# Gated delta-rule recurrence on one core: tokens loaded a round further ahead, another order on TensorE, ScalarE and GpSimd, Gram tiles with step and kind innermost

## The chip, the cores and the metric

One core of a Trainium2 chip runs the whole program. The metric is the device time of one execution in microseconds (us); lower is better. The engines are TensorE (PE; its weight loads are the row PEld), VectorE (DVE), ScalarE (ACT), GpSimd (POOL), and the queue of SyncE (SP), which issues nearly all DMAs.

## The reference, cut to what matters

The program computes four residual blocks on x of shape (4, 1024, 128) in float32: a gated delta rule (phase a), a routed expert FFN (b), banded attention (c), and two layers of local attention with FFN (d). The change touches phase a alone. Its core, for 16 heads with key and value width 64:

```
q, k, v = silu(causal_conv4(x @ W.T))      # 4 taps over time, per channel
a, beta = sigmoid(x @ Wa.T + ba), sigmoid(x @ Wb.T + bb)
def step(S, inp):
    qt, kt, vt, at, bt = inp
    err = jnp.einsum('bhij,bhj->bhi', S, kt) - vt
    S = at[..., None] * S - bt[..., None, None] * (err[..., None] * kt[:, :, None, :])
    o = jnp.einsum('bhij,bhj->bhi', S, qt)
    return (S, o)
# then: o normalised over its 64 values, times sigmoid(x @ Wg.T), times Wo
```

Each of the 1024 steps needs the state S that the step before left, so the recurrence is serial in time.

## The kernel before

**Tiling.** Time is cut into 32 segments of 32 steps (`SEG`), each into two chunks of 16 steps (`CK`). The loop of each engine runs once per segment; such a round s also makes the projections of segment s+1, the normalisation of s-1 and the gate and output of s-2. g = 2s + chunk numbers the chunks. All engines run through fixed lists (`tensor`, `scalar`, `gpsimd`, `vector`, `sync` of `DeltaRule`); semaphores hold them together. Nothing is scheduled at run time: what stands first in an engine's list goes first, and a wait holds all that stands behind it on that engine.

**VectorE's chain.** For each chunk VectorE transposes P2, the products of keys and queries with the past state, out of banks 4 and 5 (L1284), then does steps 1 to 7 (products L1319, sums L1325), transposes the first half's w into `Wt` (L1340), and waits for TensorE's `pe_cross` (L709), which multiplies Wt by the Gram values `Gx` of the first half against the second. It transposes that result into `X` (L1353), does steps 9 to 15, transposes w again (L1381) and forms the outputs `o2` (L1392). Between L1340 and L1353 it places other work: in chunk 0 the reduction of the mean (L1263), the transpose of the decay gates (L1239) and of an older o (L1273); in chunk 1 the reduction of the deviation (L1263) and the transpose of the Gram rows `G1` to `g2` (L1255). At step 4 of chunk 0 it adds half of the state (L1367).

**TensorE.** In a round: `pe_U` (L735; keys times w into the new state; batches 0 and 1, then 2 and 3 after L1284 has emptied banks 4 and 5), `pe_time_rows` (L604), projections of the gates `a` (L569), of `g` (L556), `pe_moment` (L632), `pe_cross` (L709), `pe_turn` (L614), projections of k and q (L556), `pe_past_state` (L672) and `pe_past_chunk` (L691), which together make the P2 of the next chunk, `pe_gram` (L581), `pe_next_gram` (L594), the second cross, the projection of v (L569), `pe_out` (L644), `pe_past_state`, `pe_carry` (L718), `pe_past_chunk`. Projections and Gram products go through a ring of two banks (`take`): the n-th waits until ScalarE has emptied the one two before it.

**ScalarE** empties these banks in the same order. `act_gram` copies each Gram bank three ways: 128 x 256 to `Gn` (L836), 128 x 256 of the second chunk to `G1` (L838) and four times 16 x 256 of the first chunk (L842). `G1` lies as [kind z, step t, head]; one head's steps are 16 elements (64 bytes) apart.

**GpSimd** multiplies the state by the chunk's decays (`pool_decay`, L1004, four quarters), works on the history of w, scales P2 and X (L1079 to L1105), builds running decays (`pool_cumulate`, L1138), and at the round's end prepares the next segment: `pool_gram_rows` (L1162), `pool_prepare` (L1055), `pool_values` (L1155). **SyncE** loads the tokens of segment s+1 (`xseg`, four buffers, L1418) at the start of round s, and spreads the decays over the state's layout (L1437).

Of the kernel before, what the change touches and what calls it, by code (L numbers as in the profile page):

```python
# [442 lines left out]
class DeltaRule:  # L443
# [251 lines left out]
    def pe_cross(self, e, q, s, ch):  # L695
# [25 lines left out]
    def pe_U(self, e, q, s):  # L721
# [3 lines left out]
        for pair in range(0, NB, 2):  # L725
# [14 lines left out]
    def tensor(self, e, q):  # L740
# [9 lines left out]
        for s in range(self.nseg):  # L750
            old, older, nxt, g = s - 1, s - 2, s + 1, 2 * s
            more = nxt < self.nseg
            if old >= 0:
                self.pe_U(e, q, old)
            for n in range(2):
                self.pe_time_rows(e, q, s, n)
            if more:
                for half in range(2):
                    self.pe_project_rows(e, q, "a", nxt, half)
# [6 lines left out]
            if older >= 0:  # L766
                for n in range(2):
                    self.pe_turn(e, q, older, n)
            if more:
                for part in range(2):  # L770
                    self.pe_project(e, q, "k", nxt, part)
                self.pe_project(e, q, "q", nxt, 0)
            self.pe_past_state(e, q, g + 1)
            self.pe_past_chunk(e, q, g + 1)
            if more:
                for part in range(1, 3):
                    self.pe_project(e, q, "q", nxt, part)
                for n in range(2):
                    self.pe_gram(e, q, nxt, n)
            if old >= 0:  # L780
                self.pe_moment(e, q, old, "dev")
            if more:
                for n in range(2):
                    self.pe_next_gram(e, q, s, n)
            self.pe_cross(e, q, s, 1)
            if more:
                for half in range(2):
                    self.pe_project_rows(e, q, "v", nxt, half)
            if older >= 0:
                self.pe_out(e, q, older)  # L790
            if more:
# [34 lines left out]
    def act_gram(self, e, q, s, par):  # L826

        heads = slice(8 * par, 8 * par + 8)
        v = self.held(("gram", s, par)).rearrange("p (r c t z) -> p c r z t", z=2, c=NCK, t=CK)
        dst = self.G1[:, :, :, heads].rearrange("p z t r -> p r z t")  # L830
        q.wait_ge(self.s_full, ("gram", s, par))
        if s:
# [3 lines left out]
        e.activation(self.Gn[0][:, heads, :], self.held(("gram", s, par)).rearrange("p (r x) -> p r x", r=NCT)[:, :, SEG:], ACT.Copy,  # L836
                     scale=1 / 8).then_inc(*self.s_gahead.at((s, par)))
# [40 lines left out]
    def act_gram_bank(self, e, q, g):  # L878
# [6 lines left out]
        e.activation(self.gbank[:, 0:CK - 1, 0, :], self.g2[:, 0, 1:CK, js], ACT.Copy)  # L885
# [2179 lines left out]
```

## Time and profile before

| | us |
|---|---|
| median of 3 runs | 3957.62 (3955.55 to 3961.41) |
| profiled execution | 3969.15, its span 3967.4 |
| busy in the span: PE, PEld | 3272.5, 2459.8 |
| busy: DVE, ACT, POOL | 2960.2, 2058.8, 2234.4 |

A line of the timeline view gives start and length in us, engine, line, operation, output<-inputs, shapes and count; in brackets the idle time of the engine before it and what ended it. "issue" is time in which the engine waited for nothing that the profile shows. Phase a's recurrence lies between about 150 and 2430 us of the span.

### The profile page before, as it was taken

The page shows a single profiled execution, that of the slowest core. Times are in us where ns is not written, and L with a number is a line of the kernel's source. Part 1 is how long each engine was busy: PE and PEld are TensorE (multiplying, and loading weights), DVE is VectorE, ACT ScalarE, POOL GpSimd, SP SyncE. Part 2 cuts the span into 40 slices and gives each one's busy share as a digit, 9 for nine tenths or more (in the row PEclk, how much of TensorE's full clock was granted, in tenths as well). Part 3 has the DMA queues.
Part 4 walks back from the last instruction along what each step waited for, and adds up shares of the span by engine and source line. Part 5 has one row for each costly group of instructions (what it writes and reads, how often), then busy time and mean ns, then how long its engine had stood idle before and what let it go on. Part 6 is the DMA issues. An engine that isn't in the chain of part 4 may idle for free. (4 is left out here: it accounts for less than half of the span.)

```text
span 3967.4 us, 141766 instructions
## 1 busy us (share of the span) xinstructions
PE 3272.5 (82%) x61117; PEld 2459.8 (62%) x61117; DVE 2960.2 (75%) x6533; ACT 2058.8 (52%) x4486; POOL 2234.4 (56%) x2793
## 2 busy tenths in 40 slices
PE   4688888888888888888888874769999889898989
PEld 2567666676676766666667663545666557655765
DVE  4488887877878888788888883147888878847884
ACT  2434444444444444434444432337887789828982
POOL 1367767767676777767767672431101088608860
PEclk8889999889899999889989985789999999999999
DMA  2111111111111111111011113200000011101111
GB/s 74 31 41 39 30 50 31 43 39 29 44 39 43 40 29 45 38 42 38 27 39 37 39 37 107 66 27 2 2 2 2 14 31 39 36 18 31 38 37 27
DMA packets 156019, 141.02 MB, mean 36 GB/s; under 512 B 64977, under 2 KB 108237, under 8 KB 155139
## 3 DMA queue, kind: packets, MB, share of 16 engines
q1 hardware_dynamic: 153090, 129.25, 11.9%
q8 instruction: 482, 7.90, 0.8%
q0 software_dynamic: 2304, 2.71, 0.2%
q14 instruction: 143, 1.16, 0.1%
HBM read 96.12 MB, written 16.82 MB: 28 GB/s over the span
## 5 line engine op out<-in xcount | busy, mean ns | idle before, releaser
L1319 DVE TENSOR_TENSOR a_tmp<-a_h,banks 128x128 f32<-128x128 f32 (+6 forms) x896 | 435.6, 486 | 28.8 <-DVE a_h L1294 0.2
L1325 DVE TENSOR_REDUCE a_h<-a_tmp 128x64 f32<-128x128 f32 (+6 forms) x896 | 432.0, 482 | 8.8
L1004 POOL TENSOR_TENSOR a_st<-a_st,a_ab 128x512 f32<-128x512 f32 x252 | 315.2, 1278 | 0.0
L813 ACT ACTIVATE a_kq<-banks 128x512 f32<-128x512 f32 (+2 forms) x160 | 88.9, 556 | 400.8 <-PE banks L556 400.8
L556 PE MATMUL banks<-a_xseg,a_w_k 128*128 128x128 f32 x2048 | 250.4, 284 | 50.9 <-ACT a_oT L919 33.6
L556 PEld LDWEIGHTS banks<-a_xseg,a_w_k 128*128 128x128 f32 x2048 | 244.3, 200 | 58.2 <-ACT a_oT L919 40.5
L2198 ACT ACTIVATE c_s<-c_s,c_low 128x384 f32<-128x384 f32 (+1 forms) x512 | 266.3, 579 | 18.9 <-DVE c_low L2142 13.5
L1019 POOL TENSOR_TENSOR a_h<-a_h,a_a 128x128 f32<-128x128 f32 (+3 forms) x256 | 141.2, 551 | 226.5 <-DVE a_h L1325 223.3
L2142 DVE CUSTOM_DVE_ANT_0 c_s<-banks,c_band 128x384 f32<-128x384 f32 (+1 forms) x512 | 245.5, 517 | 23.6 <-PE banks L2067 23.6
L2243 POOL TENSOR_TENSOR c_qm<-c_qT,c_heads 128x512 f32<-128x512 f32 x32 | 33.3, 1040 | 396.1 <-PE banks L2067 395.8
L556 PE MATMUL banks<-a_xseg,a_w_q 128*128 128x128 f32 x2048 | 242.8, 275 | 3.3 <-issue 3.3
L569 PE MATMUL banks<-a_w_v,a_xseg 128*32 128x512 f32 x2048 | 240.9, 623 | 1.2 <-ACT a_va L822 1.2
L2081 PE MATMUL banks<-k_ident,c_s 128*128 128x128 f32 x1408 | 216.6, 283 | 28.6 <-ACT c_pt L2205 15.8
L556 PEld LDWEIGHTS banks<-a_xseg,a_w_q 128*128 128x128 f32 x2048 | 233.9, 191 | 6.5 <-issue 3.6
L2081 PEld LDWEIGHTS banks<-k_ident,c_s 128*128 128x128 f32 x1408 | 154.3, 142 | 119.8 <-ACT c_s L2198 113.6
L822 ACT ACTIVATE a_va<-banks 128x512 f32<-128x512 f32 x128 | 138.4, 1108 | 172.1 <-PE banks L569 172.0
L2579 ACT ACTIVATE d_S<-d_S,d_low 128x128 f32<-128x128 f32 x512 | 199.2, 399 | 19.0 <-DVE d_low L2644 18.6
L2428 PE MATMUL banks<-d_wqkv,d_hT 128*128 128x512 f32 x384 | 198.8, 632 | 11.3 <-DVE d_rot L2626 6.8
L709 PE MATMUL banks<-a_wt,a_gx 32*32 32x64 f32 x8192 | 182.3, 259 | 25.9 <-DVE a_wt L1340 18.4
L1323 DVE TENSOR_TENSOR a_h<-a_h,banks 128x32 f32<-128x32 f32 (+6 forms) x640 | 175.1, 274 | 22.0
L709 PEld LDWEIGHTS banks<-a_wt,a_gx 32*32 32x32 f32 x8192 | 168.5, 149 | 36.3 <-issue 31.2
L2719 POOL TENSOR_TENSOR d_sw<-d_raw,d_tab 128x256 f32<-128x256 f32 x256 | 178.4, 729 | 0.0
(326 smaller groups left out, 8961.0 us busy)
## 6 DMA issues: line engine op xcount, KB each, us to landing
a_ab<-decays SPq DMA_DIRECT2D x512, 128.0 KB, 3.0
d_Vs<-d_V SPq DMA_DIRECT2D x128, 128.0 KB, 2.4
sent<-k_nothing SPq DMA_DIRECT2D x40, 64.5 KB, 2.6
b_xe<-sent SPq DMA_DIRECT2D x8, 322.5 KB, 3.5
a_xseg<-xn SPq DMA_DIRECT2D x32, 70.0 KB, 2.5
a_xrow<-in_L_attn_x SPq DMA_DIRECT2D x128, 16.0 KB, 1.8
x<-a_xrow SPq DMA_DIRECT2D x128, 16.0 KB, 2.1
back<-k_nothing SPq DMA_DIRECT2D x32, 64.0 KB, 1.6
```

The costliest lines, as they stand in the source:

```text
L556: t = e.matmul(b[:, m * SW:(m + 1) * SW].rearrange("p (b t) -> p b t", b=NB), self.wT[n][:, j, ct * P:(ct + 1) * P], xs[:, :, off:off + SE ...
L569: t = e.matmul(b[bi * SEG:(bi + 1) * SEG, :], xs[:, bi, off:off + SEG], self.wT[n][:, j, part], start=(j == 0), stop=(j == taps - 1))
L709: t = e.matmul(xb[rows, at:at + DK], self.Gx[rows, :, :, 8 * par + ct].rearrange("p z t -> p (z t)"), self.Wt[rows, x:x + 2, :].rearrange( ...
L1004: e.tensor_tensor(sv, sv, self.ab[:, 8 * n:8 * n + 8, :], ALU.mult).then_inc(*self.s_decay.at((g, n)))
L1319: e.tensor_tensor(prod, both, gram, ALU.mult).then_inc(*step.at((g, t, "product")))
L1325: e.tensor_reduce(self.results(ch, t), prod, AX.X, ALU.add).then_inc(*step.at((g, t, "w")))
L2081: t = e.transpose(b[:, j * P:(j + 1) * P], self.S[u % self.NS][:, j * P:(j + 1) * P], self.c.ident[:])
L2142: e.tensor_tensor_reduce(out=self.S[u % self.NS][:, 0:w], in0=self.c.bank(r)[:, 0:w], in1=self.W.band[:, m0:m0 + w], scale=-HD ** -0.5, sc ...
L2198: e.activation(s[:, 0:w], s[:, 0:w], ACT.Exp, scale=-1.0, bias=self.low[u % self.NS][:, 0:1]).then_inc(*self.s_exp.at(u))
L2428: e.matmul(b, self.hT[:, g * P:(g + 1) * P], self.W.wqkv[:, z * INNER:(z + 1) * INNER], start=True, stop=True).then_inc(*self.s_proj.at((g ...
L2579: t = e.activation(s, s, ACT.Exp, scale=-1.0, bias=self.low[g % 2][:, par, r:r + 1], accum_out=self.rows[g % 2][:, par, r:r + 1])
L2719: e.tensor_tensor(self.heads(sw[:, z, :])[:, :, a * hf:(a + 1) * hf], self.heads(raw[:, z, :])[:, :, (1 - a) * hf:(2 - a) * hf], sn, ALU.m ...
```

## The change

1. **Loads.** SyncE loads segment 1 at once and then segment s+2 in round s, behind the first spread of decays, where it loaded s+1 at the round's start.
2. **TensorE.** The two halves of the `a` projection stand between and behind the two halves of `pe_U`, ahead of the time rows. k's two parts alternate with `pe_turn`; `pe_past_state` of the second chunk goes ahead of the first part of q. The deviation's moment goes ahead of the Gram product; `pe_out` and the second cross go ahead of `pe_next_gram`.
3. **ScalarE** follows with the same order.
4. **Layout.** `G1`, `Gx` become [head, t, z] and `g2` [t, z, column], `X` [.., t, z]: ScalarE writes runs of 32, and the cross reads its 32 weights as one run. VectorE's L1255 reads heads 32 elements apart.
5. **GpSimd.** All four decays of the second chunk stand ahead of `pool_cross`; two of them stood behind it. Two steps of `pool_cumulate` move from ahead of it to behind `pool_query`.

```diff
-            self.G1, self.g2 = sb("g1", [P, 2, CK, H0]), sb("g2", [P, 2, CK, SEG])
-            self.Gx, self.X = sb("gx", [P, 2, CK, H0]), sb("cross", [P, 32, 2 * CK])
+            self.G1, self.g2 = sb("g1", [P, H0, CK, 2]), sb("g2", [P, CK, 2, SEG])
+            self.Gx, self.X = sb("gx", [P, H0, CK, 2]), sb("cross", [P, 32, CK, 2])
...
-                    t = e.matmul(xb[rows, at:at + DK], self.Gx[rows, :, :, 8 * par + ct].rearrange("p z t -> p (z t)"),
+                    t = e.matmul(xb[rows, at:at + DK], self.Gx[rows, 8 * par + ct].rearrange("p t z -> p (t z)"),
...
             if old >= 0:
-                self.pe_U(e, q, old)
+                self.pe_U(e, q, old, (0,))
+            if more:
+                self.pe_project_rows(e, q, "a", nxt, 0)
+            if old >= 0:
+                self.pe_U(e, q, old, (2,))
+            if more:
+                self.pe_project_rows(e, q, "a", nxt, 1)
             for n in range(2):
                 self.pe_time_rows(e, q, s, n)
-            if more:
-                for half in range(2):
-                    self.pe_project_rows(e, q, "a", nxt, half)
...
             self.pe_cross(e, q, s, 0)
-            if older >= 0:
-                for n in range(2):
+            for n in range(2):
+                if more:
+                    self.pe_project(e, q, "k", nxt, n)
+                if older >= 0:
                     self.pe_turn(e, q, older, n)
+            self.pe_past_state(e, q, g + 1)
             if more:
-                for part in range(2):
-                    self.pe_project(e, q, "k", nxt, part)
                 self.pe_project(e, q, "q", nxt, 0)
-            self.pe_past_state(e, q, g + 1)
             self.pe_past_chunk(e, q, g + 1)
             if more:
                 for part in range(1, 3):
                     self.pe_project(e, q, "q", nxt, part)
-                for n in range(2):
-                    self.pe_gram(e, q, nxt, n)
             if old >= 0:
                 self.pe_moment(e, q, old, "dev")
             if more:
                 for n in range(2):
-                    self.pe_next_gram(e, q, s, n)
+                    self.pe_gram(e, q, nxt, n)
+            if older >= 0:
+                self.pe_out(e, q, older)
             self.pe_cross(e, q, s, 1)
             if more:
+                for n in range(2):
+                    self.pe_next_gram(e, q, s, n)
                 for half in range(2):
                     self.pe_project_rows(e, q, "v", nxt, half)
-            if older >= 0:
-                self.pe_out(e, q, older)
...
-        v = self.held(("gram", s, par)).rearrange("p (r c t z) -> p c r z t", z=2, c=NCK, t=CK)
-        dst = self.G1[:, :, :, heads].rearrange("p z t r -> p r z t")
+        v = self.held(("gram", s, par)).rearrange("p (r c x) -> p c r x", r=NCT, c=NCK)
+        dst = self.G1[:, heads].rearrange("p r t z -> p r (t z)")
...
             if more:
-                for n in range(2):
+                for n in range(4):
                     self.pool_decay(e, q, g, n)
-                self.pool_cumulate(e, q, nxt, 3, 5)
             self.pool_cross(e, q, s, 1)
             self.pool_first_half(e, q, s, 1)
             if more:
                 self.pool_past(e, q, s)
-                for n in range(2, 4):
-                    self.pool_decay(e, q, g, n)
             self.pool_query(e, q, s, 1)
             if more:
-                self.pool_cumulate(e, q, nxt, 5, HC)
+                self.pool_cumulate(e, q, nxt, 3, HC)
...
-        rows = self.G1[:].rearrange("p z t (h o) -> p (z t) h o", o=1).broadcast_to([P, 2 * CK, H0, 2])
-        e.transpose(self.g2[:].rearrange("p z t j -> p (z t) j"), rows).then_inc(*self.s_g2.at(s))
+        rows = self.G1[:].rearrange("p (h o) t z -> p (t z) h o", o=1).broadcast_to([P, 2 * CK, H0, 2])
+        e.transpose(self.g2[:].rearrange("p t z j -> p (t z) j"), rows).then_inc(*self.s_g2.at(s))
...
         self.load(e, 0)
+        self.load(e, 1)
         self.put_decays(e, q, 0)
         self.spread_decays(e, q, 0)
         for s in range(self.nseg + 2):
-            if s + 1 < self.nseg:
-                if s >= 3:
-                    q.wait_ge(self.s_full, ("g", s - 3, 1))
-                self.load(e, s + 1)
             if s >= 2:
                 self.get_rows(e, q, s - 2)
             self.fill.piece(e, s)
             if s < self.nseg:
                 self.spread_decays(e, q, 2 * s + 1)
+            if s + 2 < self.nseg:
+                if s >= 2:
+                    q.wait_ge(self.s_full, ("g", s - 2, 1))
+                self.load(e, s + 2)
             if s + 1 < self.nseg:
                 self.put_decays(e, q, s + 1)
                 self.spread_decays(e, q, 2 * s + 2)
```

The other edits follow from these: ScalarE's list, and the views of `g2` and `X` in the new layouts with the same elements.

## Rows read from the trace of the kernel before

**Rows 1.** The page, busy us (share of the span) xinstructions

```profile
PE 3272.5 (82%) x61117; PEld 2459.8 (62%) x61117; DVE 2960.2 (75%) x6533; ACT 2058.8 (52%) x4486; POOL 2234.4 (56%) x2793
```

**Rows 2.** Windows view, 30 rounds: length, busy us by engine, PEclk, DMA share, GB/s

```profile
218.10:2341.70 2123.60, 1769.41 (x44976) 1417.29 (x44965) 1731.89 (x3210) 931.86 (x1581) 1521.19 (x2036) 0.92 0.13 38
```

**Rows 3.** Waits of VectorE from 160 to 2400 us: total us, times, longest

```profile
DVE a_cross L1353 <- PE banks L709: 117.8, 35, 4.3
DVE a_g L1255 <- ACT a_g L842: 75.6, 31, 3.8
DVE a_p L1284 <- PE banks L691: 74.9, 33, 4.3
DVE a_mom L1263 <- PE banks L632: 61.1, 27, 5.2
```

**Rows 4.** Timeline of VectorE, chunk 1 of round 12, chunk 0 of round 13

```profile
1030.47 1.25 DVE L1284 STREAM_TRANSPOSE a_p<-banks 128x1024 f32<-128x1024 f32 x1 [2.48 <-PE banks L691]
...
1040.13 2.05 DVE L1340 STREAM_TRANSPOSE a_wt<-a_h 128x1024 f32<-128x1024 f32 x1
...
1044.67 1.25 DVE L1255 STREAM_TRANSPOSE a_g<-a_g 128x1024 f32<-128x1024 f32 x1 [2.41 <-ACT a_g L842]
1049.40 1.25 DVE L1353 STREAM_TRANSPOSE a_cross<-banks 128x1024 f32<-128x1024 f32 x1 [3.49 <-PE banks L709]
...
1064.14 2.46 DVE L1392 TENSOR_TENSOR a_o<-a_p,a_h 128x512 f32<-128x512 f32 x1
1066.70 1.25 DVE L1284 STREAM_TRANSPOSE a_p<-banks 128x1024 f32<-128x1024 f32 x1
...
1082.72 0.29 DVE L1263 TENSOR_REDUCE a_mom<-banks 128x32 f32<-128x128 f32 x1 [3.06 <-PE banks L632]
...
1085.21 1.21 DVE L1353 STREAM_TRANSPOSE a_cross<-banks 128x1024 f32<-128x1024 f32 x1
...
1098.71 1.10 DVE L1392 TENSOR_TENSOR a_o<-a_p,a_h 128x512 f32<-128x512 f32 x1
1101.21 1.25 DVE L1284 STREAM_TRANSPOSE a_p<-banks 128x1024 f32<-128x1024 f32 x1 [1.40 <-PE banks L691]
```

**Rows 5.** Timeline of TensorE in the same stretch

```profile
1029.80 0.63 PE L691 MATMUL banks<-a_wt,a_gn 32*32 32x64 f32 x27 [1.39 <-issue]
1030.36 5.62 PE L556 MATMUL banks<-a_xseg,a_w_q 128*128 128x128 f32 x48
...
1045.70 3.64 PE L709 MATMUL banks<-a_wt,a_gx 32*32 32x64 f32 x128
...
1063.17 2.02 PE L691 MATMUL banks<-a_wt,a_gn 32*32 32x64 f32 x128
...
1068.01 1.98 PE L735 MATMUL banks<-a_wt,a_kt 32*64 32x64 f32 x64 [1.72 <-DVE a_p L1284]
...
1075.04 3.40 PE L569 MATMUL banks<-a_w_a,a_xseg 128*32 128x512 f32 x16 [1.48 <-DMA a_xseg<-xn]
...
1082.61 2.06 PE L709 MATMUL banks<-a_wt,a_gx 32*32 32x64 f32 x128
```

**Rows 6.** Timeline of ScalarE, one Gram bank emptied

```profile
1037.84 0.39 ACT L836 ACTIVATE a_gn<-banks 128x256 f32<-128x256 f32 x1 [1.30 <-PE banks L581]
1038.12 0.62 ACT L838 ACTIVATE a_g<-banks 128x256 f32<-128x256 f32 x1
1038.78 2.48 ACT L842 ACTIVATE a_g<-banks 16x256 f32<-16x256 f32 x4
```

**Rows 7.** Timeline of GpSimd, second half of chunk 1

```profile
1042.63 2.48 POOL L1004 TENSOR_TENSOR a_st<-a_st,a_ab 128x512 f32<-128x512 f32 x2
...
1050.73 0.57 POOL L1092 TENSOR_TENSOR a_cross<-a_cross,a_dk 128x128 f32<-128x128 f32 x1 [4.32 <-DVE a_cross L1353]
...
1063.66 2.39 POOL L1155 TENSOR_TENSOR a_bv<-a_bv,a_beta 128x1024 f32<-128x1024 f32 x1
```

**Rows 8.** Windows view, TensorE alone, during the cross of 1045.70 us

```profile
1045.70:1049.30 3.60, 3.60 (x138) 0.50 0.02 5
```

More of the change, by code:

```diff
@@ L719, in pe_carry, with pe_U @@
                      start=True, stop=False).then_inc(*self.s_carried.at((s, n)))
-    def pe_U(self, e, q, s):
+    def pe_U(self, e, q, s, pairs):
         q.wait_ge(self.s_evac, ("rows", s, 1))
         q.wait_ge(self.s_wt, 2 * s + 1)
-        for pair in range(0, NB, 2):
+        for pair in pairs:
             if pair:
@@ L835, in act_gram @@
             q.wait_ge(self.s_p, 2 * s - 1)
-        e.activation(self.Gn[0][:, heads, :], self.held(("gram", s, par)).rearrange("p (r x) -> p r x", r=NCT)[:, :, SEG:], ACT.Copy,
-                     scale=1 / 8).then_inc(*self.s_gahead.at((s, par)))
+        e.activation(self.Gn[0][:, heads, :], v[:, 1], ACT.Copy, scale=1 / 8).then_inc(*self.s_gahead.at((s, par)))
         e.activation(dst, v[:, 1], ACT.Copy, scale=-1 / 8).then_inc(*self.s_gwhole.at((s, par)))
@@ L952, in scalar @@
                     self.act_project_rows(e, q, "a", nxt, half)
+            for n in range(2):
+                self.act_time_rows(e, q, s, n)
             if older >= 0:
@@ L955, in scalar @@
                     self.act_gate(e, q, older, n)
-                for n in range(2):
+            for n in range(2):
+                if more:
+                    self.act_project(e, q, "k", nxt, n)
+                if older >= 0:
                     self.act_affine(e, q, older, n)
             if more:
-                for part in range(2):
-                    self.act_project(e, q, "k", nxt, part)
                 self.act_project(e, q, "q", nxt, 0)
@@ L971, in scalar @@
                     self.act_gram(e, q, nxt, n)
+            if older >= 0:
+                self.act_out(e, q, older)
+            if more:
                 for n in range(2):
@@ L1104, in pool_query @@
         q.wait_ge(self.s_cross, (g, "decayed"))
-        e.tensor_tensor(of_q[:, :, last], of_q[:, :, last], self.X[:, :, CK + last], ALU.subtract).then_inc(*self.s_pq.at(g))
+        e.tensor_tensor(of_q[:, :, last], of_q[:, :, last], self.X[:, :, last, 1], ALU.subtract).then_inc(*self.s_pq.at(g))
     def pool_gate(self, e, q, s, half):
@@ L1159, in pool_gram_rows @@
         for ch in range(NCK):
-            v = self.g2[:, 0, :, ch * CK:(ch + 1) * CK]
+            v = self.g2[:, :, 0, ch * CK:(ch + 1) * CK]
             bc = self.beta8[:, s * SEG + ch * CK:s * SEG + (ch + 1) * CK].rearrange("p (t o) -> p t o", o=1).broadcast_to([P, CK, CK])
             e.tensor_tensor(v, v, bc, ALU.mult).then_inc(*self.s_bg.at((s, ch, "beta")))
-            flat = self.g2[:].rearrange("p z t j -> p z (t j)")
-            own = ch * CK + SEG + 1
+            flat, row = self.g2[:].rearrange("p t z j -> p (t z j)"), 2 * SEG
+            of_k, of_q = row + ch * CK + 1, SEG + ch * CK + 1
             q.wait_ge(self.s_bg, (s, ch, "beta"))
-            e.memset(flat[:, 0, own:own + (CK - 2) * (SEG + 1) + 1:SEG + 1], 1.0).then_inc(*self.s_bg.at((s, ch, "one")))
-            e.memset(flat[:, 1, own - SEG:own - SEG + (CK - 2) * (SEG + 1) + 1:SEG + 1], 0.0).then_inc(*self.s_bg.at((s, ch)))
+            e.memset(flat[:, of_k:of_k + (CK - 2) * (row + 1) + 1:row + 1], 1.0).then_inc(*self.s_bg.at((s, ch, "one")))
+            e.memset(flat[:, of_q:of_q + (CK - 2) * (row + 1) + 1:row + 1], 0.0).then_inc(*self.s_bg.at((s, ch)))
     def gpsimd(self, e, q):
@@ L1352, in dve_cross @@
             q.wait_ge(self.s_pq, g - 1)
-        e.transpose(self.X[:], self.c.bank(6, 2).rearrange("p (x i) -> p i x", i=32)).then_inc(*self.s_xt.at(g))
+        e.transpose(self.X[:].rearrange("p i t z -> p i (t z)"), self.c.bank(6, 2).rearrange("p (x i) -> p i x", i=32)).then_inc(*self.s_xt.at(g))
         q.wait_ge(self.s_xt, g)
```

15 lines of the change are left out of this document (5 added, 10 removed).

## The prediction

> **What bounds it now.** I read the page's busy line first [rows 1]: TensorE 3272.5 and VectorE 2960.2 us lead, but these are sums over four phases, and the change touches one. The windows view of 30 rounds of it [rows 2] gives 2123.60/30 = 70.8 us a round, VectorE busy 1731.89/30 = 57.7, TensorE 59.0 at a mean granted clock of 0.92, GpSimd 50.7, ScalarE 31.1. So nothing is saturated: the round is a serial chain through VectorE, and what counts is what VectorE waits for. The waits view [rows 3] names four: 117.8 us for the cross, 75.6 for ScalarE's Gram copies, 74.9 for the past chunk, 61.1 for the mean: 329.4 us in 31 rounds, 10.6 a round. The VectorE timeline shows where they lie. Call the starts of L1284 and L1353 D0, X0 in chunk 0 and D1, X1 in chunk 1. Chunk 1 of round 12 [rows 4]: D1 = 1030.47 after 2.48 us of waiting, X1 = D1 + 18.93, of which 2.41 + 3.49 are waits, next D0 = D1 + 36.23. Chunk 0 of round 13: X0 = D0 + 18.51 with 3.06 of waiting for the mean, D1 = D0 + 34.51 with 1.40. The pattern repeats in all middle rounds; the mean's wait swings from 0.5 to 5.2.
>
> **The change, part by part.**
>
> *D0 to X0.* TensorE reaches the mean late: it stands 1.72 us before the second half of U and 1.48 before the `a` rows, which last 3.40, for a DMA [rows 5]. Between U's halves half of the `a` rows (3.40/2 = 1.7) now fills the gap, and tokens issued a round earlier have long landed: together some 3.2 us, against a wait of 3.06. ScalarE's copies out of the ring come in the same new order, so nothing queues in front of them. With the mean early, VectorE's own work sets X0: 18.51 - 3.06 = 15.45. The mean wait (61.1/30 = 2.0 a round) goes. What is late next is the cross: it can't start before L1340 ends, at about D0 + 12.9, and if the clock has fallen in TensorE's new gap before it, it takes 3.64 as in the other chunk and not the 2.06 of this one [rows 5], and X0 slips to D0 + 16.6. I take half of that: **-2.05 + 0.5**. SyncE's added wait (for an old g) holds only the load, the decays' write and the spreads behind it; those wait for GpSimd 39 us at worst anyway, so nothing.
>
> *X0 to D1.* VectorE needs 14.6 us from X0 to be free (1098.71 + 1.10 - 1085.21) [rows 4]. The past chunk starts when L1381 ends, X0 + 12.8, and takes some 2.05, so X0 + 14.85 is possible, a wait of 0.25. It was 2.48 at 1030.47 (about 2.3 on average): 1.39 of "issue" inside the past chunk [rows 5], where 256 small products with their weight loads follow on each other, and the rest of 0.84 by TensorE coming late out of k, q and past state. Now q's first part (1.95) stands between the two, as the carry does ahead of the other chunk, whose past chunk runs its 128 products without such a stop in 2.02 at 1063.17 [rows 5]. With the gaps above filled and k alternating with the turns, TensorE is no longer late. From 2.3 to between 0.25 and 1.6 (the stop stays); I take 0.65: **-1.65**.
>
> *D1 to X1.* ScalarE's Gram bank takes 3.42 now (0.28 + 0.66 + 2.48) [rows 6]. The copy to `Gn`, of the same 256 elements in runs, lasts 0.39 and the next starts 0.28 behind it, where the scattered one lasts 0.62. At that pace a bank is 0.28 + 0.41 + 4 x 0.31 = 1.9 to 2.0; bounds are 3.42 (no gain) and 1.6. From D1: q's parts end at 5.5 [rows 5], the moment 2.05 later, the Grams at 8.5 and 9.45, ScalarE's copies at 10.7 and 12.7 against 14.15 now. That is where VectorE, free at D1 + 11.9, waits 0.8 and no longer 2.4. L1255 (1.25) then ends at 14.0. The cross today starts at 15.2, behind the next Grams, for which ScalarE's copies must have emptied both banks, and at a granted clock of 0.50 takes 3.64 [rows 5, 8]. Ahead of it now stand only Grams and out (2.05), dense work up to D1 + 11.5; it starts with L1340's end at 11.8 and ends at 13.9 warm, 15.4 at half clock. X1 = 14.0 to 15.4 for 18.93; I take 14.3: **-4.6**. L1255 reads heads 128 bytes apart now. The transpose of the cross, with a source stepped as widely but in a bank, takes 1.25, L1340, which writes that way, 2.05 [rows 4]: a price of 0 to 0.8; it is nearer to L1353, as a read, and I put it at nothing.
>
> Here a rule bears. ScalarE's steps of 64 bytes cost 0.62 for 0.39 [rows 6]. The Trainium skill (SBUF — State Buffer, Door 1: The DMA port swizzle) says that SBUF has 16-byte lines, that each access crossing into a new one pays, and that two hits per line are wanted. By it the copies gain, the trace agrees, but L1255 would pay; with L1340's 2.05 X1 is 14.8 and the total 15 us higher. It reads each element twice, which may be the two hits.
>
> *X1 to the next D0.* VectorE needs 14.75 to the start of L1392; that takes 2.46 for 1.10 elsewhere, ending 0.55 behind GpSimd's L1155 (1063.66 + 2.39) [rows 4, 7]. GpSimd is what is late next. It is free of second-half work at D1 + 12.15 and today idles 4.32 us before L1092 [rows 7]. Now four decays (4 x 1.25) end at D1 + 17.2, the cross product is ready at 18.25, and step 12 on VectorE asks for it at X1 + 5.0 = 19.3: covered by 1.0. The rest of its list up to L1155's end is as now, 1050.73 to 1065.98 less two decays plus two cumulates: 15.25 - 2.5 + 1.35 = 14.1. So L1155 ends at D1 + 31.3, and L1392, asked for at 29.05, ends at 31.9 rather than the 31.5 of today's spacing: **+0.4**. ScalarE's copies of v were ready 3.9 us before VectorE took them (1058.26 to 1062.13); the next Grams, about 1.9 of TensorE, now come between cross and v and leave 2.0 of that. The root, behind out and next Grams on ScalarE, is done about 1 us before L1268 asks, an estimate from the same spacings.
>
> *Sum.* -2.05 + 0.5 - 1.65 - 4.6 + 0.4 = -7.4 a round, 63.4 us for 70.8. Rounds 0 to 30 have it: 31 x 7.4 = 229. The last has no next segment, and phases b to d are as before. Against the profiled execution 3969.15 - 229 = 3740; it lies 11.5 above the median of the runs, so I put **3957.6 - 229 = 3729 us**. Floor: all 10.6 of waits but 0.25 + 0.8 a round go, 9.5 x 31 = 295, 3663.
>
> **Rivals.**
> 1. *GpSimd takes VectorE's place.* Its list from D1 + 12.15 on has no idle left. If VectorE's two-input instructions and its own hold each other up as L1392 shows, its end slips by some 2 us: +62, 3791. For: the 2.46 and a cover of only 1.0 at step 12. Against: 4.32 idle today is more than what moves ahead. The Trainium skill (SBUF — State Buffer, Who interferes with whom) tells of a lock for whole instructions between GpSimd and a VectorE instruction with two SBUF inputs; the trace agrees by the 1.36 us of L1392.
> 2. *The copies don't speed up* (what costs isn't the step). Then the Grams are out at D1 + 15.5, X1 = 16.75, 2.45 x 31 = 76 more: 3805. Against: rows 6.
> 3. *TensorE binds in part*: cold crosses in both chunks (0.6 and 1.1 more than taken) and the stop that stays (1.0): 2.7 x 31 = 84, 3813. For: two stretches at half clock are there now. Against: they follow gaps, and the gaps are filled.
> 4. *Slower: TensorE's clock.* At full clock its list is some 57 us a round. If the mixed small products kept a share f of it at 1.2 GHz, the round would be 57 x (1 + f): it decides from f = 0.24, 70.8 us. With a third it is 76, +5.2 x 31: 4119. Against: filling gaps has raised the clock in every dense stretch here.
>
> **How the numbers follow.** Forecast (within 3663 to 3760) 0.60; rival 1 0.14; rival 2 0.06; rival 3 0.12; rival 4 0.03; a loss elsewhere that eats all of it 0.02; better than the floor, by VectorE's instructions meeting GpSimd's less, 0.03. The range 3655 to 3840 leaves out rival 4, half of the better case and what rivals 1 to 3 give together. A measurement of this kernel tells 0.2% (8 us) from no change: faster 0.94, within 0.02, slower 0.04.
>
> **What would show it.** Right: the waits of L1353, L1255, L1284 and L1263 for TensorE and ScalarE fall from 329 to some 90 us; L838 and L842 at 0.38; the cross of chunk 1 at clock 1.00; no DMA wait of the `a` rows; GpSimd's idle before L1092 near nothing. Wrong: L1255 at 2 us; L1319 at step 12 waiting for L1094; L1294 waiting for L1155; the clock of the window below 0.85.

## The result, and the profile after

The changed kernel takes **3811.05 us** (median, 3801.64 to 3818.85) beside 3956.59 for the kernel before on the same chips: a ratio of 0.9632, 95% interval 0.9606 to 0.9658, or 146 us less. Forecast were 3729 in a range of 3655 to 3840: the sign, the range and most of the mechanism held, but over a third of the forecast gain is missing, and the time lies above the 3663 to 3760 to which the prediction gave its main chance of 0.60. The profiled execution took 3810.68 with a span of 3808.9; the profiled kernel before had 3967.4.

The windows view, 30 rounds from D0 of round 1 to D0 of round 31, as in [rows 2] (length, busy us of each engine, granted clock, DMA share, GB/s):

```profile
214.90:2185.10 1970.20, 1721.63 (x45024) 1363.01 (x45024) 1768.69 (x3209) 852.69 (x1581) 1536.13 (x2036) 0.94 0.14 41
```

A round is 1970.20/30 = 65.7 us for 70.8. The reader should see two things. ScalarE is busy 79 us less and TensorE 48 less, as wanted. But VectorE, with the same instructions, is busy **36.8 us more** (1768.69 for 1731.89): some of them have become longer.

The waits view of VectorE, 160 to 2300 us (us in total, times, longest), against [rows 3]:

```profile
DVE a_cross L1353 <- PE banks L709: 61.2, 43, 3.8
DVE a_g L1255 <- ACT a_g L843: 22.3, 31, 2.0
DVE a_st L1367 <- issue: 20.1, 9, 3.2
...
DVE a_p L1284 <- PE banks L691: 17.8, 28, 2.0
DVE a_mom L1263 <- PE banks L632: 15.6, 3, 14.3
DVE a_mom L1268 <- ACT a_mom L899: 7.1, 8, 1.3
```

The four old waits fell from 329.4 to 116.9 us, of which 14.3 is one wait after the last round: 212 us less. Only 158.5 of the span was gained. The difference is in new waits (L1367 20.1, L1268 7.1, and L1247 5.6 for ScalarE's copies of v) and in the longer instructions. The lines view by shape shows those (busy us, mean ns | idle before), first before, then after:

```profile
L1358 DVE TENSOR_TENSOR a_h<-a_p,a_cross 128x128 f32<-128x128 f32 x64 | 27.4, 429 | 2.3
L1289 DVE TENSOR_TENSOR a_p<-a_p,a_dk 128x128 f32<-128x128 f32 x64 | 20.1, 314 | 2.2
L1355 DVE TENSOR_TENSOR a_cross<-a_cross,a_dk 128x128 f32<-128x128 f32 x64 | 18.7, 292 | 2.2
```

```profile
L1358 DVE TENSOR_TENSOR a_h<-a_p,a_cross 128x128 f32<-128x128 f32 x64 | 43.2, 675 | 2.2
L1289 DVE TENSOR_TENSOR a_p<-a_p,a_dk 128x128 f32<-128x128 f32 x64 | 35.3, 552 | 2.2
L1355 DVE TENSOR_TENSOR a_cross<-a_cross,a_dk 128x128 f32<-128x128 f32 x64 | 32.9, 514 | 2.2
```

The same work costs 15.8 + 15.2 + 14.2 = 45 us more; other instructions became a little shorter, which leaves the 36.8. VectorE's timeline of chunk 1 in round 16 shows where (start, length), and GpSimd's beside it shows why:

```profile
1231.76 1.25 DVE L1284 STREAM_TRANSPOSE a_p<-banks 128x1024 f32<-128x1024 f32 x1
1233.05 1.12 DVE L1289 TENSOR_TENSOR a_p<-a_p,a_dk 128x128 f32<-128x128 f32 x1
...
1246.41 1.25 DVE L1353 STREAM_TRANSPOSE a_cross<-banks 128x1024 f32<-128x1024 f32 x1 [0.58 <-PE banks L709]
1247.70 0.89 DVE L1355 TENSOR_TENSOR a_cross<-a_cross,a_dk 128x128 f32<-128x128 f32 x1
1248.62 1.26 DVE L1358 TENSOR_TENSOR a_h<-a_p,a_cross 128x128 f32<-128x128 f32 x1
...
1264.84 1.25 DVE L1284 STREAM_TRANSPOSE a_p<-banks 128x1024 f32<-128x1024 f32 x1
```

```profile
1231.06 2.96 POOL L1116 TENSOR_TENSOR a_y<-a_oT,a_og 128x512 f32<-128x512 f32 x2
...
1244.71 5.03 POOL L1007 TENSOR_TENSOR a_st<-a_st,a_ab 128x512 f32<-128x512 f32 x4
```

L1289 ends at 1234.17, 0.15 after GpSimd's gate products (1231.06 + 2.96); L1358 ends at 1249.88, 0.14 after the four decays (1244.71 + 5.03 = 1249.74). All three have both inputs in SBUF. In the kernel before GpSimd was idle when L1355 and L1358 came (L1092 waited 4.32 us there [rows 7]), and L1289 of chunk 1 came when the gate products were over: it took 0.30 us on average, and now 0.81.

The table gives the four parts of a round as means of rounds 1 to 30, worked out from the timeline view of VectorE of each profile by the starts of L1284 (D0 in chunk 0, D1 in chunk 1) and L1353 (X0, X1). The forecast row is the row of before with the terms of the prediction's sum; the kernels below the changed one are those of the experiments:

| us | X0 - D0 | X0 to D1 | X1 - D1 | X1 to D0 | round |
|---|---|---|---|---|---|
| before | 17.51 | 16.95 | 18.96 | 17.36 | 70.8 |
| forecast | 15.95 | 15.3 | 14.3 | 17.8 | 63.4 |
| **changed** | 16.82 | 15.27 | 14.99 | 18.59 | 65.7 |
| layout_only | 17.00 | 16.75 | 16.72 | 17.53 | 68.0 |
| order_only | 16.65 | 15.40 | 16.41 | 17.48 | 65.9 |
| old_last | 16.36 | 15.25 | 16.77 | 17.22 | 65.6 |
| old_first | 16.47 | 15.02 | 15.05 | 18.51 | 65.1 |
| old_loads | 20.84 | 14.95 | 15.06 | 18.57 | 69.4 |
| old_gpsimd | 16.76 | 15.11 | 14.94 | 17.65 | 64.5 |
| three_decays | 16.55 | 15.17 | 14.83 | 18.30 | 64.9 |
| centre_early | 16.78 | 15.85 | 14.34 | 18.42 | 65.4 |
| both | 16.62 | 15.98 | 14.50 | 18.18 | 65.3 |
| shift64 | 16.75 | 15.37 | 14.70 | 18.67 | 65.5 |
| add_late | 16.19 | 15.07 | 14.99 | 18.64 | 64.9 |
| best | 16.52 | 15.05 | 15.00 | 17.30 | 63.9 |

The decisive column is the last but one: X1 came 4 us earlier, and the way from there to D0 became 1.2 us longer. By instruction, in us a round: L1358 +0.52, L1355 +0.47, the wait of L1268 +0.22 and that of L1247 +0.19, less 0.26 of L1392.

### The profile page after: what moved, and what is told of

The parts are those of the page before. It is cut to its first block and busy times, and to the rows that moved or that the text cites. A ratio compares the mean times of both kernels' runs of the same rounds, so it can differ in the third digit from the quotient of the medians.

```text
span 3808.9 us, 141737 instructions
## 1 busy us (share of the span) xinstructions
PE 3221.9 (85%) x61117; PEld 2401.6 (63%) x61117; DVE 2996.8 (79%) x6533; ACT 1974.1 (52%) x4486; POOL 2251.0 (59%) x2793
## 3 DMA queue, kind: packets, MB, share of 16 engines
HBM read 96.12 MB, written 16.82 MB: 30 GB/s over the span
## 5 line engine op out<-in xcount | busy, mean ns | idle before, releaser
L1319 DVE TENSOR_TENSOR a_tmp<-a_h,banks 128x128 f32<-128x128 f32 (+6 forms) x896 | 435.4, 486 | 28.8 <-DVE a_h L1294 0.2
L556 PE MATMUL banks<-a_xseg,a_w_k 128*128 128x128 f32 x2048 | 260.6, 287 | 26.6 <-DMA a_xseg<-xn 18.2
L569 PE MATMUL banks<-a_w_v,a_xseg 128*32 128x512 f32 x2048 | 263.0, 658 | 7.3 <-issue 7.0
L709 PE MATMUL banks<-a_wt,a_gx 32*32 32x64 f32 x8192 | 156.2, 236 | 129.5 <-DVE a_wt L1340 110.0
L709 PEld LDWEIGHTS banks<-a_wt,a_gx 32*32 32x32 f32 x8192 | 143.5, 119 | 142.5 <-issue 141.4
## 6 DMA issues: line engine op xcount, KB each, us to landing
sent<-k_nothing SPq DMA_DIRECT2D x40, 64.5 KB, 2.5
```

What stands on the lines that cost most here:

```text
L556: t = e.matmul(b[:, m * SW:(m + 1) * SW].rearrange("p (b t) -> p b t", b=NB), self.wT[n][:, j, ct * P:(ct + 1) * P], xs[:, :, off:off + SE ...
L569: t = e.matmul(b[bi * SEG:(bi + 1) * SEG, :], xs[:, bi, off:off + SEG], self.wT[n][:, j, part], start=(j == 0), stop=(j == taps - 1))
L709: t = e.matmul(xb[rows, at:at + DK], self.Gx[rows, 8 * par + ct].rearrange("p t z -> p (t z)"), self.Wt[rows, x:x + 2, :].rearrange("p h i ...
L1319: e.tensor_tensor(prod, both, gram, ALU.mult).then_inc(*step.at((g, t, "product")))
```

## The experiments

**Theory (lock).** The waits went about as forecast, and most of what is missing was lost where VectorE's instructions with two SBUF inputs now meet GpSimd's: the one that comes second is held until the other has ended. **Rivals:** TensorE's order or its stops took it; or GpSimd's list as a whole binds.

layout_only, order_only, old_last and old_gpsimd ran on one chip, three_decays, centre_early, both and old_loads on a second, shift64, old_first, add_late and best on a third, so within such a group the times can be compared directly. shift64 is the changed kernel but for some products ahead of the first round, and stands for it on its chip (3808.16 us, 3802.82 to 3811.19).

### Layout alone, order alone

layout_only is the kernel before with the new layouts of `G1`, `Gx`, `g2` and `X`; order_only is the changed kernel with the old ones.

```diff
-            self.G1, self.g2 = sb("g1", [P, H0, CK, 2]), sb("g2", [P, CK, 2, SEG])
+            self.G1, self.g2 = sb("g1", [P, 2, CK, H0]), sb("g2", [P, 2, CK, SEG])
```

> The kernel before with nothing but the new layout of the Gram tiles and of X. Theory A (VectorE's chain sets the time, and the layout takes the wait for the Gram copies by itself): ScalarE's copies fall to 0.38 us each, the next Grams and so the cross of chunk 1 start earlier too, X1 falls from D1 + 18.9 to between 14.4 and 15.9, mean wait and chunk 0 stay: -3.5 us a round, about 3850 us. Theory B (the order of TensorE's last part is what brings X1 down): X1 stays above 17, 3900 us or more. L1255 stays at 1.25 us by the first, goes to 2.0 if wide steps in SBUF cost a transpose.

Measured: 3881.93 us, ratio 0.9833 (0.9812 to 0.9854). In the changed kernel the copies L839 and L843 take 0.38 and 0.37 us for 0.63 and 0.60, and L1255, which now reads at 128 bytes a step, still 1.25. The wait for the copies nearly vanishes with the layout alone, but the one for the cross stays at 112.7:

```profile
DVE a_cross L1352 <- PE banks L709: 112.7, 35, 4.7
DVE a_p L1283 <- PE banks L691: 63.7, 32, 3.8
DVE a_mom L1262 <- PE banks L632: 45.9, 26, 3.7
DVE a_g L1254 <- ACT a_g L841: 5.4, 8, 1.2
```

X1 is D1 + 16.72: between what the two theories said, and the 3850 us was too low by 32.

> The changed kernel with the old layout. The Gram copies last 3.4 us a bank again, so L1255 ends at about D1 + 16.8 and X1 is there, 1.9 us later than in the changed kernel. Lock theory (VectorE's L1355 and L1358, two inputs in SBUF, are held by GpSimd's decays, which end at D1 + 17.5): they come behind the decays now and fall back to 0.29 and 0.43, which gives 1.4 us back: 0.5 us a round more than the changed kernel, about 3825 us. Without the lock (TensorE or fetch stops took the missing gain): the full 1.9 a round, about 3870 us.

Measured: 3815.85 us, ratio 0.9655 (0.963 to 0.968), within the error of the changed kernel. The Grams' copies cost 96.1 us of waiting again, and X1 is 1.4 later, where 1.9 was expected. But L1355 and L1358 come when the decays are over:

```profile
1250.07 1.25 DVE L1256 STREAM_TRANSPOSE a_g<-a_g 128x1024 f32<-128x1024 f32 x1 [2.98 <-ACT a_g L844]
1251.24 1.21 DVE L1354 STREAM_TRANSPOSE a_cross<-banks 128x1024 f32<-128x1024 f32 x1
1252.48 0.29 DVE L1356 TENSOR_TENSOR a_cross<-a_cross,a_dk 128x128 f32<-128x128 f32 x1
1252.81 0.43 DVE L1359 TENSOR_TENSOR a_h<-a_p,a_cross 128x128 f32<-128x128 f32 x1
```

and X1 to D0 is 17.48 for 18.59. So 1.4 us gained by the layout and 1.1 us lost to GpSimd are the same microsecond: the new layout, worth 1.7% alone, adds next to nothing on top of the order. The lock theory's 3825 was missed by 9 us, the rival's 3870 by 54.

### TensorE's last part as before

```diff
+            if more:
+                for n in range(2):
+                    self.pe_gram(e, q, nxt, n)
             if old >= 0:
                 self.pe_moment(e, q, old, "dev")
             if more:
                 for n in range(2):
-                    self.pe_gram(e, q, nxt, n)
+                    self.pe_next_gram(e, q, s, n)
+            self.pe_cross(e, q, s, 1)
+            if more:
+                for half in range(2):
+                    self.pe_project_rows(e, q, "v", nxt, half)
             if older >= 0:
                 self.pe_out(e, q, older)
-            self.pe_cross(e, q, s, 1)
             if more:
-                for n in range(2):
-                    self.pe_next_gram(e, q, s, n)
-                for half in range(2):
-                    self.pe_project_rows(e, q, "v", nxt, half)
```

(ScalarE's `act_out` goes back behind v too.)

> The changed kernel with the last part of TensorE's and ScalarE's round as before (Gram, deviation, next Gram, cross, v, out). Theory A (with the fast copies this order hardly matters): next Gram waits for ScalarE until D1 + 11.4, the cross ends at 14.4 to 15.9, X1 like the 15.0 of the changed kernel, 3800 to 3835 us. Theory B (the order is what counts): X1 near 17 to 19, 3880 us or more.

Measured: 3808.97 us, ratio 0.9633 (0.9607 to 0.966): no different from the changed kernel, as theory A had it in total. Its reason was wrong, though: X1 - D1 is 16.77 and not 15. The cross is waited for longer, and most of what this costs comes back behind X1, 17.22 for 18.59, where the decays are out of the way (the rest lies in D0 to X0, 16.36 for 16.82):

```profile
DVE a_cross L1355 <- PE banks L709: 131.2, 51, 4.4
```

It is the same exchange as in order_only.

### GpSimd's list as before

```diff
             if more:
-                for n in range(4):
+                for n in range(2):
                     self.pool_decay(e, q, g, n)
+                self.pool_cumulate(e, q, nxt, 3, 5)
             self.pool_cross(e, q, s, 1)
             self.pool_first_half(e, q, s, 1)
             if more:
                 self.pool_past(e, q, s)
+                for n in range(2, 4):
+                    self.pool_decay(e, q, g, n)
             self.pool_query(e, q, s, 1)
             if more:
-                self.pool_cumulate(e, q, nxt, 3, HC)
+                self.pool_cumulate(e, q, nxt, 5, HC)
```

> The changed kernel with GpSimd's list of before: two decays and two steps of the running decays ahead of the cross product, two decays behind. Lock theory: GpSimd is idle when L1355 and L1358 come, they last 0.29 and 0.43 and not 0.89 and 1.26; X1 to the start of L1392 falls from 16.2 to 14.8, -1.2 to -1.4 us a round, about 3770 us: faster than the changed kernel. Rival (the decays ahead of the crossing help, or GpSimd's whole list binds): 3811 or slower.

Measured: 3777.43 us, ratio 0.9578 (0.955 to 0.9606): undoing this part of the change makes it faster. The interval just touches that of the changed kernel; on the same chip all four times (3774.00 to 3793.22) lie below those of old_last (3795.34 to 3811.04) and order_only. The same place in VectorE's and GpSimd's timelines:

```profile
1227.73 0.29 DVE L1358 TENSOR_TENSOR a_cross<-a_cross,a_dk 128x128 f32<-128x128 f32 x1
1228.06 0.60 DVE L1361 TENSOR_TENSOR a_h<-a_p,a_cross 128x128 f32<-128x128 f32 x1
```

```profile
1224.74 2.50 POOL L1007 TENSOR_TENSOR a_st<-a_st,a_ab 128x512 f32<-128x512 f32 x2
1227.20 1.31 POOL L1141 TENSOR_TENSOR a_dc<-a_dc,a_a 128x128 f32<-128x128 f32 x2
```

VectorE's two products (L1358 and L1361 here) take 0.89 us together for 2.15. They still meet the running decays, but each of these lasts 0.66 us, where a decay of the state lasts 1.25: who has to wait, waits for a short one. Over 30 rounds the two give 0.85 us a round.

Another 0.48 comes from L1392 (L1395 here), whose mean in chunk 1 falls from 2.20 to 1.72, and this shows the lock from both sides. In the changed kernel GpSimd's L1158 starts 0.08 us after VectorE's L1247, whose result it reads, has ended, in all 30 rounds, and L1392, which comes 0.71 us later, ends 0.55 us after L1158. VectorE itself releases the instruction that then blocks it; round 16:

```profile
1260.53 1.21 DVE L1247 STREAM_TRANSPOSE a_bv<-a_va 128x1024 f32<-128x1024 f32 x1
1262.54 2.19 DVE L1392 TENSOR_TENSOR a_o<-a_p,a_h 128x512 f32<-128x512 f32 x1
```

```profile
1261.62 0.30 POOL L1060 COPY a_dk<-a_beta 128x64 f32<-128x64 f32 x1
1261.83 2.36 POOL L1158 TENSOR_TENSOR a_bv<-a_bv,a_beta 128x1024 f32<-128x1024 f32 x1
```

This also answers the rival that GpSimd's whole list binds: L1158 waits for VectorE there, with GpSimd idle for up to 2.4 us before it. With GpSimd's old list VectorE comes first in 12 of 30 rounds. L1395 then takes 0.69 to 0.78, and GpSimd's instruction is the one that is stretched (0.83 for 0.30). Round 4:

```profile
466.19 0.69 DVE L1395 TENSOR_TENSOR a_o<-a_p,a_h 128x512 f32<-128x512 f32 x1
```

```profile
466.22 0.83 POOL L1060 COPY a_dk<-a_beta 128x64 f32<-128x64 f32 x1
466.94 2.37 POOL L1158 TENSOR_TENSOR a_bv<-a_bv,a_beta 128x1024 f32<-128x1024 f32 x1
```

Some of it is lost again: the past chunk is waited for 0.26 us longer at D0, so X1 to D0 is 0.94 shorter and not 1.3.

> The changed kernel with three of chunk 1's decays ahead of GpSimd's cross product and one behind. Lock theory: the third decay ends about when L1353 does, so L1355 and L1358 fall from 0.74 and 0.92 to 0.29 and 0.43, GpSimd's list stays as long and as dense: 3770 to 3785 us, like the kernel with GpSimd's old list. Rival (the two steps of the running decays, not the decays, made the difference there): 3805 to 3811 us.

Measured: 3790.03 us, ratio 0.9607 (0.9572 to 0.9643), between the two expectations. L1358 is back at 0.43 (mean over chunk 1), L1355 still at 0.69: in the rounds in which the cross comes late both are free (0.29 and 0.42 in round 15, X1 at D1 + 17.3), in the others the third decay still reaches into L1355. The interval overlaps that of the changed kernel, so by its time alone this run would not decide. Its durations show that the fourth decay was what held L1358. They also show where this went: L1392 of chunk 1 now starts within 0.1 us of L1158 in most rounds, mostly second, and takes 2.47 for 2.20, so X1 to D0 is only 0.3 shorter.

### Moving GpSimd's centring into its idle time

```diff
             if old >= 0:
                 self.pool_clear(e, q, old)
+                for n in range(2):
+                    self.pool_centre(e, q, old, n)
             self.pool_cross(e, q, s, 0)
...
-            if old >= 0:
-                for n in range(2):
-                    self.pool_centre(e, q, old, n)
```

> The changed kernel with GpSimd's two centring products in its idle time ahead of chunk 0's cross product. Lock theory: the gate products end 2.5 us earlier and no longer meet L1289 of chunk 1, which falls from 0.78 to 0.30 us; L1392 of chunk 0 may meet the gates instead: -0.3 to -0.5 us a round, 3795 to 3802 us. Rival (GpSimd's list doesn't matter there): 3811 us.

Measured: 3806.42 us, ratio 0.9659 (0.9617 to 0.9701): nothing gained. L1289 of chunk 1 is at 0.29 as expected. But GpSimd's centring often still runs when L1355 and L1358 of **chunk 0** come (in round 4 both are held until a centring product ends). These two, 0.29 and 0.43 in the changed kernel, have means of 0.53 and 0.72; X0 to D1 is 15.85 for 15.27, X1 - D1 14.34 for 14.99. The meeting was moved, not removed.

> Both edits of GpSimd's list, three decays ahead and centring early, in the changed kernel. If the two lock costs add: 3755 to 3770 us. If VectorE is then stopped by something else (the root, v, the past chunk): 3775 to 3785 us.

Measured: 3796.69 us, ratio 0.9616 (0.9578 to 0.9655). Slower than the 3775 to 3785 of the worse of the two expectations, and no faster than three_decays alone; L1355 and L1358 of chunk 0 are held as in centre_early (0.58 and 0.82).

### The loads as before

```diff
+            if s + 1 < self.nseg:
+                if s >= 3:
+                    q.wait_ge(self.s_full, ("g", s - 3, 1))
+                self.load(e, s + 1)
             if s >= 2:
                 self.get_rows(e, q, s - 2)
```

(and the early load of segment 1 and that of s+2 go)

> The changed kernel with the loads of the kernel before: segment s+1 loaded at the start of round s. The first half of the a rows stands ahead of the second half of U now, so its wait for the load holds U, and with it VectorE's L1367 at step 4, which asks at D0 + 4.7. The load lands near D0 + 8 (issued behind the output rows): 3 to 5 us a round, 3900 to 3960 us. Rival (a load has landed in time anyway, or VectorE isn't held): 3811 to 3830 us.

Measured: 3930.36 us, ratio 0.9949 (0.9925 to 0.9972). The waits of VectorE, then of TensorE:

```profile
DVE a_st L1367 <- issue: 158.5, 30, 7.8
```

```profile
PE banks L569 <- DMA a_xseg<-xn: 160.3, 31, 7.8
```

The 160 us that the `a` rows wait for the DMA reach VectorE whole, through the half of U behind them. With this order the early load is worth some 120 us, and without it the change is nearly nothing. With the old order it had 44 us of DMA wait on TensorE to remove; no run has the early load alone.

### TensorE's first part as before, with the early loads

```diff
-                self.pe_U(e, q, old, (0,))
-            if more:
-                self.pe_project_rows(e, q, "a", nxt, 0)
-            if old >= 0:
-                self.pe_U(e, q, old, (2,))
-            if more:
-                self.pe_project_rows(e, q, "a", nxt, 1)
+                self.pe_U(e, q, old, (0, 2))
             for n in range(2):
                 self.pe_time_rows(e, q, s, n)
+            if more:
+                for half in range(2):
+                    self.pe_project_rows(e, q, "a", nxt, half)
```

(ScalarE's list follows.)

> The changed kernel with TensorE's and ScalarE's first part as before: U whole, time rows, then both a rows. Theory A: what brings the mean in time is mostly the early load; U's waits for TensorE stops stay or shrink, the mean waits 0 to 1 us: +0 to +0.5 a round, 3805 to 3830 us. Theory B (the filled gap and the warmer clock matter): time rows at half clock again, the mean waits 2 us as before, 3860 to 3880 us.

Measured: 3794.76 us, ratio 0.9625 (0.9584 to 0.9666). Theory A, and 10 us below its range. The mean waits 0.78 us a round (chunk 0), L1367 only 0.06 and the cross 0.35, for 0.04, 0.73 and 0.92. So filling the gap between U's halves took the mean's wait from 0.78 to 0.04 and lost more than that in the other two; the early load brought most of it, from 2.04 to 0.78. On the same chip all four times (3786.42 to 3797.99) lie below those of shift64: the new first part costs some 13 us.

### L1367 and TensorE's stops

The changed kernel's TensorE stops in round 16 inside the first half of U, for no reason that the profile shows (start, length, count, idle before):

```profile
1199.29 0.92 PE L735 MATMUL banks<-a_wt,a_kt 32*64 32x64 f32 x47
1202.09 0.46 PE L735 MATMUL banks<-a_wt,a_kt 32*64 32x64 f32 x17 [1.88 <-issue]
1202.48 1.53 PE L569 MATMUL banks<-a_w_a,a_xseg 128*32 128x512 f32 x8
1203.94 1.99 PE L735 MATMUL banks<-a_wt,a_kt 32*64 32x64 f32 x64
```

Ahead of L735's second half the `a` rows' half stands now, so the stop reaches L1367, which waits 2.0 us in this round. Counted over the trace, the products with their loads between two such stops are close to whole multiples of 128 pairs: 128, 383, 1020, 765, 383 and 382 between neighbouring ones around round 16. Of the 68 stops of over 0.5 us in the recurrence none is more than 9 pairs short of such a multiple from the next, and some matmul records are missing from a trace. The page has 482 instruction packets of 16 KB.

> The changed kernel with 64 extra matmuls with their weight loads (128 instructions) on TensorE ahead of the first round; their result is read by nobody. Fetch theory: the stops named issue come at every so many 128 pairs of TensorE's program, so they move by 64 pairs to other instructions: the rounds in which L1367 waits (4, 7, 12, 16, 19, 20, 24, 28, 29 in the changed kernel) become others, and the sum stays within some 15 us, 3800 to 3830 us. Rival (a stop belongs to an instruction or to DMA traffic at that moment): the same rounds wait.

Measured: 3808.16 us, ratio 0.9659 (0.9619 to 0.9699). The page counts 128 matmuls more, not 64: each of the written ones became two. So the program was shifted by 256 instructions, and the stop of round 16 came at the same place:

```profile
1195.76 0.92 PE L735 MATMUL banks<-a_wt,a_kt 32*64 32x64 f32 x47
1198.81 0.62 PE L735 MATMUL banks<-a_wt,a_kt 32*64 32x64 f32 x17 [2.13 <-issue]
```

If the stops come at multiples of 128 pairs, a shift by 128 must leave them where they are; if they belong to the instruction, too. This run couldn't tell, but the traces of the other kernels can. Counted from TensorE's first product, the first such stop of the recurrence falls on place 74 to 77 of a block of 128 in ten kernels, before, changed, layout_only, old_last and best among them, and none is more than 10 pairs short of a whole multiple of 128 from the next, though these kernels have other instructions at those places: before stops mostly inside L691, L735 and L672, the changed kernel inside L594, L735 and L709. So a stop belongs to a place in the program and not to an instruction. shift64's page also has one instruction packet more, 483, for its 256 instructions. That the stops are the fetch of these packets is supported by this, not shown. The Trainium skill (Runtime: NRT & Kernel Launch, Instruction fetch mechanics) says that code comes in blocks of 256 instructions and that crossing into one is mostly hidden. The spacing agrees with it, and "mostly hidden" does by count: in 30 rounds there are some 350 such blocks, and 68 stops of over 0.5 us in the recurrence of the changed kernel, up to 2.4.

> The changed kernel with VectorE's two additions into the state (L1367) at step 6 of chunk 0 and not at step 4. Nobody asks for them before the mean at about D0 + 9. The stops of TensorE inside U (L1367 waits 20 to 22 us in nine rounds) are covered by 2.5 us more: L1367's wait falls below 5 us, 3790 to 3798 us. Rival: the time returns in L1353's wait, because TensorE is late there too in those rounds: 3803 to 3811 us.

```diff
+            if t == HAND + 2 and ch == 0 and s:
+                self.dve_add(e, q, s - 1)
             if t == HAND:
-                if ch == 0 and s:
-                    self.dve_add(e, q, s - 1)
                 q.wait_ge(self.s_rest, (g, "sub", 1))
```

Measured: 3791.79 us, ratio 0.9627 (0.9588 to 0.9667). L1367 waits 0.09 us a round for 0.73, and X0 - D0 is 16.19 for 16.82: the wait doesn't come back in L1353's (0.47 for 0.92), only in part in the mean's (0.46 for 0.04). In the profile the round is 0.8 us shorter. The interval of the ratio overlaps that of the changed kernel, but beside shift64 on the same chip all four times are lower (3787.09 to 3798.84), by 16 us: the wait for U's stops was a cost.

### A faster version

best is the changed kernel with GpSimd's old list, the additions at step 6 and ScalarE's root ahead of the next Grams.

> The changed kernel with GpSimd's old list, the additions at step 6 and ScalarE's root ahead of the next Grams. If the gains add (34 us of the list, up to 15 of L1367, up to 7 of L1268): 3750 to 3765 us. If VectorE's next wait takes them: 3775 us.

Measured: 3758.44 us, ratio **0.9535** (0.9495 to 0.9574), a further 1% below the changed kernel, whose interval it doesn't touch. Beside shift64 it is 50 us, of which add_late alone has 16. The intervals of best and old_gpsimd overlap, so what the root's place is worth no time shows; L1268's wait is gone (0.00 for 0.22 a round). L1392 of chunk 1 comes ahead of L1158 in 16 of 30 rounds and has a mean of 1.48.

```profile
213.70:2129.70 1916.00, 1690.67 (x44931) 1335.79 (x44934) 1739.58 (x3210) 852.33 (x1579) 1534.43 (x2036) 0.96 0.14 42
```

A round is 63.9 us, and VectorE's busy time in 30 rounds, 1739.58, is back to within 8 us of before. That is a balance: L1292 (L1289 in the changed kernel) still takes 0.62 and 0.96 in the two chunks for 0.29 and 0.30 before, one us a round that best has left.

## Why the prediction was right, and by how much not

- **The number.** Every term but one came out short, and the time is inside the range because the range reached over the rivals. It lies nearest to the 3805 and 3813 of rivals 2 and 3, of which only a part of rival 3 happened (chunk 0's cross). Of the 2.3 us a round that are missing (65.7 for 63.4) L1289, L1355 and L1358 took 1.5, where the prediction had allowed for 0.4 in all, at L1392; L1367 took 0.7.
- **What bounds the kernel.** Right: the four waits fell by 212 us, and 158.5 us of the span went with them.
- **D0 to X0**, forecast 15.95, measured 16.82. The mean is in time (0.04 of waiting for 2.04), but old_first shows that the early load brought most of that (0.78), and that filling the gap cost more than it gave. The step that failed is the sentence that named only the cross as late next. Half of U is late too: the prediction moved an `a` half ahead of it and did not ask who waits for that half. L1367 does, 0.73 us a round. The cross at falling clock was foreseen, with half a microsecond; its wait rose from 0.12 to 0.92, and it lasts over 2.5 us in 16 of 30 rounds, where one did before. In round 17, after 3.44 us without work, 128 products and a stop stretch over 4.7 us at a mean granted clock of 0.53:

```profile
1277.80:1282.50 4.70, 3.73 (x128) 0.53 0.03 7
```

- **X0 to D1**, forecast 15.3, measured 15.27. The stop inside the past chunk is gone as reasoned: 74.9 us of waiting became 17.8. The stops went elsewhere, mostly behind the second cross (L594: 47.7 us in 30 stops).
- **D1 to X1**, forecast 14.3, measured 14.99. ScalarE's copies came out at the figure (0.37 for 0.38), the cross of chunk 1 lasts 1.99 us in the median round for 3.64, in round 16 at clock 1.00:

```profile
1244.35:1246.30 1.95, 1.95 (x129) 1.00 0.03 8
```

  0.5 of the 0.7 missing is L1289, held by the gate products that D1 now comes early enough to meet.
- **X1 to D0**, forecast +0.4, measured +1.23. This is the term that was mis-sized. The prediction took L1392 for the only place where the two engines meet and put the loss there; that one shrank (2.45 to 2.20 in chunk 1). It showed GpSimd's idle 4.32 us before L1092 as room to fill, and did not look at what VectorE does in that gap. Its path to D0 was another too: it had GpSimd's list end at D1 + 31.3 by itself, and L1158 waited for VectorE's L1247 instead and ended at D1 + 32.8. The two smaller covers were misread as well: L1268 and L1247, which should have had 1 and 2 us to spare, wait 0.22 and 0.19. Rival 1 had the mechanism and 2 us as its price, but at the wrong instructions.
- **The length of L1392.** The prediction read chunk 0's 1.10 us as its own length. In the last round, with GpSimd idle, it is 0.69:

```profile
2243.45 0.69 DVE L1392 TENSOR_TENSOR a_o<-a_p,a_h 128x512 f32<-128x512 f32 x1
```

  In rounds 2 to 30 GpSimd's L1125 or L1158 (L1122 and L1155 before) is running when it comes, and L1392 ends 0.55 after it. Before and after the change alike this costs 2.1 to 2.2 us a round (an estimate from the means of 1.11 and 2.45, 1.31 and 2.20 less 0.69 each), more than the three products that drew attention.
- **What each part was worth.** The prediction did not price the layout and the order apart. layout_only and order_only show 1.7 and 3.5% alone, and the changed kernel has 3.7; the prediction followed one path for both and so did not see that the order alone would bring nearly all of it.
- **Steps of 64 bytes.** ScalarE's copies fell from 0.63 and 0.60 to 0.38 and 0.37 us when their writes went from steps of 64 bytes to runs; their reads in the bank went from steps of 8 bytes to runs with them, and no run separates the two. The transpose that reads at 128 bytes costs nothing (1.25 both times). The Trainium skill (SBUF — State Buffer, Door 1: The DMA port swizzle) says that each access which crosses into a new 16-byte line pays. The copies agree with it and the transpose doesn't, unless its double reads are the two hits, which no run shows.
- **The lock.** The Trainium skill (SBUF — State Buffer, Who interferes with whom) says that whoever of the two comes first has the port for its whole instruction and the other is blocked. The traces agree from both sides (L1395 and L1060 above), and it was the larger matter.
- **Taken for granted and wrong**: that VectorE's instructions keep their lengths. Its busy time rose by 37 us, and best got most of it back.

## What to carry to other kernels

An engine that waits is not only losing time, it is out of the others' way: before filling GpSimd's idle time or pulling VectorE's work forward, list VectorE's instructions with two SBUF inputs and see which of them will now start while GpSimd works; long GpSimd instructions there cost most. To know what an instruction costs by itself, look for one that the other engine leaves alone, in a first or last round. When two edits shorten the same wait, price them together, not one after the other. An instruction list that is moved ahead of another inherits its waiters: with the `a` rows ahead of half of U, the early load here carried 3% of the time.

## What the runs showed of the hardware

VectorE products with both inputs in SBUF that meet a running GpSimd instruction last until 0.14 to 0.15 us past its end (L1289 and L1355, 0.29 alone, up to 1.43; L1358, 0.43 alone, up to 1.26), L1392, 0.69 alone, until 0.55 past it. The one that starts first is not stretched: in round 6 of the changed kernel GpSimd's L1095 starts 0.05 us after L1355, which keeps its 0.29. Transposes, sums, and products with one input in a bank keep their lengths beside GpSimd (L1319 of 128x512: 0.69). TensorE stops of 0.5 to 2.4 us without a cause in the profile come at whole multiples of 128 matmuls with their loads. 1.95 us of large ones were put between two groups of small ones, and the stops inside the second group went (L691: 30.4 us in 27 stops before, 0.7 in 3 after) while others appeared at the next Grams; no run has that edit alone.
